# A left-shifted copy of the image: made on chip by POOL from the rows already loaded, in place of a second load

## The reference

```python
x = x + _L0_conv_ref(_gn(x), ...)   # normalise each channel, 3x3 depthwise conv with weights
                                    # chosen per image (softmax of 4 kernels), a sigmoid gate, 1x1 conv
x = x + _L1_conv_ref(_gn(x), ...)   # normalise, 1x1 conv to 192 channels, 3x3 depthwise, 8x8 FFT
                                    # product of q and k, layer norm, times v, 1x1 conv
```

## Time and profile before

| what | value |
|---|---|
| median of three runs | 3041.64 us (3037.79 to 3047.04) |
| the profiled execution's own time | 3043.07 us, of which 3041.0 us from the first to the last instruction |
| mean granted TensorE clock | 0.961 of full speed |
| PE, PEld, DVE, ACT, POOL busy | 88%, 55%, 67%, 73%, 19% |
| first stage | to about 676 us, 16 slots with a convolution |
| share of "DMA arena<-x_in" in the chain that ended last | 8% |

### The profile page before, as it was taken

How to read it: one execution, slowest core, us unless ns; L and a number is a source line. 1 busy time by engine, 2 the same in 40 slices (tenths; PEclk the granted TensorE clock), 3 DMA queues, 4 the chain that set the end, 5 groups by cost and what they waited for, 6 DMA issues and landing times.

```text
span 3041.0 us, 74966 instructions
## 1 busy us (share of the span) xinstructions
PE 2679.8 (88%) x28031; PEld 1676.5 (55%) x28031; DVE 2039.6 (67%) x3469; ACT 2219.4 (73%) x4445; POOL 574.6 (19%) x307
## 2 busy tenths in 40 slices
PE   2777777779999999999999999999999999999998
PEld 1222222226666666666666666666666666666665
DVE  7666666644767676666666667676666767676766
ACT  2455555558878787878787878787787878787885
POOL 4000000010222222222222222222222222222222
PEclk9898888879999999999999999999999999999999
DMA  9899999982222222223222222222222222222221
GB/s 190 203 283 276 287 271 270 270 212 66 59 59 58 59 58 59 69 63 72 62 69 63 68 59 58 59 58 59 59 58 59 58 59 58 59 58 59 58 58 42
DMA packets 43485, 313.88 MB, mean 103 GB/s; under 512 B 12913, under 2 KB 13050, under 8 KB 29658
## 3 DMA queue, kind: packets, MB, share of 16 engines
q1 hardware_dynamic: 43082, 308.58, 40.7%
HBM read 206.81 MB, written 101.72 MB: 101 GB/s over the span
## 4 chain that ended last, share of the span: by engine, by line
PE 60%; DVE 14%; ACT 9%; DMA 8%; issue 8%; SPq 1%; ACTq 0%; DVEq 0%; POOL 0%; POOLq 0%
PE bank L614 15%; PE bank L696 14%; PE bank L676 8%; DMA arena<-x_in 8%; PE bank L627 6%; PE bank L687 5%; PE bank L599 5%; PE bank L636 4%; DVE arena L1110 3%; ACT arena L862 3%; PE bank L562 2%; DVE arena L1130 2%; ACT arena L764 2%; DVE arena L1194 1%; DVE arena L1124 1%
## 5 line engine op out<-in xcount | busy, mean ns | idle before, releaser
L862 ACT ACTIVATE arena<-bank 64x256 f32<-64x256 f32 x2048 | 773.2, 378 | 141.0 <-PE bank L687 122.3
L486 POOL TENSOR_TENSOR arena<-arena 128x8 f32<-128x8 f32 x256 | 515.5, 2014 | 1833.8 <-DVE arena L1132 1833.7
L614 PE MATMUL bank<-arena 128*64 128x512 f16 x4608 | 715.2, 401 | 45.3 <-issue 45.3
L805 ACT ACTIVATE arena<-bank 100x512 f32<-100x512 f32 x1024 | 585.5, 639 | 105.5 <-PE bank L599 103.2
L1194 DVE TENSOR_TENSOR arena<-bank,arena 128x512 f32<-128x512 f32 x512 | 354.5, 692 | 455.4 <-ACT arena L862 410.4
L696 PE MATMUL bank<-arena 100*128 100x128 f32 x4096 | 590.0, 286 | 0.0
L696 PEld LDWEIGHTS bank<-arena 100*128 100x128 f32 x4096 | 495.8, 191 | 82.5 <-issue 82.5
L599 PEld LDWEIGHTS bank<-arena 128*64 128x64 f16 (+1 forms) x8192 | 340.4, 106 | 254.3 <-ACT arena L805 48.8
L599 PE MATMUL bank<-arena 128*64 128x128 f16 (+1 forms) x8192 | 414.4, 223 | 21.4 <-ACT arena L805 17.9
L562 PE MATMUL bank<-arena 128*32 128x512 f32 x3072 | 413.1, 679 | 4.7 <-DVE arena L986 4.0
L821 ACT ACTIVATE arena<-bank,arena 128x256 f32<-128x256 f32 x512 | 261.3, 561 | 138.5 <-PE bank L627 135.8
(11 more groups left out here) (122 smaller groups left out, 2133.1 us busy)
## 6 DMA issues: line engine op xcount, KB each, us to landing
arena<-xn_d SPq DMA_DIRECT2D x128, 536.2 KB, 8.9
xn_d<-arena SPq DMA_DIRECT2D x130, 260.0 KB, 14.1
arena<-x_in SPq DMA_DIRECT2D x64, 512.0 KB, 25.6
x_d<-arena SPq DMA_DIRECT2D x64, 512.0 KB, 14.7
arena<-x_d SPq DMA_DIRECT2D x128, 256.0 KB, 4.9
out<-arena SPq DMA_DIRECT2D x128, 256.0 KB, 4.4
arena<-x_in SPq DMA_DIRECT2D x16, 2047.9 KB, 26.9
arena<-spectra_in SPq DMA_DIRECT2D x1, 1152.0 KB
```

Of the source, the lines that this page charges most:

```text
L486: pool.tensor_tensor(tiny["rstd"][:, slot], tiny["var_eps"][:, slot], powers, ALU.pow).then_inc(s_root, 1)
L614: mm = pe.matmul(v_banks[chunk % 3][64 * s:64 * s + 64, :], v_w[:, 64 * tap:64 * tap + 64], at(xs[half], row * WP + 32 * k + dx, [32 * WP, ...
L805: act.activation(h_rows[0:WIN, :, first:first + 4], banks[g % ring][0:WIN, :].rearrange("p (i c) -> p c i", i=4), ACT.Copy).then_inc(s_h_r ...
L862: ins = act.activation(at(q_sb[n % 4][64 * to:64 * to + 64, :], 128 * half, [256, 2], [1, 128]), src, ACT.Copy)
```

## The change

The left load (`load_left`, its semaphores and its two issues on SP) is gone. POOL now waits for the middle load of `after` before it takes the root of `after`, and behind that root it makes the left-shifted copy itself: eight instructions of 16 rows by 127 columns over 32 partitions, from partitions 32 to 63 at one element further to partitions 64 to 95. The first is a multiplication by a row of ones, a two-input instruction, and the other seven are plain copies. Each adds one to `s_left_copied`. DVE's wait ahead of the edge memset (L1082) is for all eight in place of the left load. On POOL the copies stand behind the root of `after` and, in the first slot of all, behind `clear(1)`.

```diff
-        s_x3_left_in = [semaphore(f"x3_left_in{s}") for s in range(2)]
+        s_left_copied = semaphore("left_copied")
...
-            def load_left(b, n, s):
-
-                sp.dma_start(x3[s][64:96, W:W + PIX - 1], x[b].rearrange("c h w -> c (h w)")[:, 1:PIX]).then_inc(s_x3_left_in[s], 16)
...
                 if prev is not None:
-                    if after is not None:
-                        load_left(*after)
-                    elif here is not None:
+                    if after is None and here is not None:
                         load_transforms()
-                    else:
+                    elif after is None:
                         load_first_half()
                 elif after is not None:
                     b, n, s = after
                     load_middle(*after)
-                    load_left(*after)
...
                 if after is not None:
-                    root(after[0], 1)
+                    b, n, s = after
+                    pool.wait_ge(s_x3_mid_in[s], 16 * (n + 1))
+                    root(b, 1)
                     if prev is None and here is None:
                         clear(1)
+                    for i in range(8):
+                        first = (1 + 16 * i) * W
+                        dst, src = at(x3[s][64:96, :], first, [W, 16], [1, W - 1]), at(x3[s][32:64, :], first + 1, [W, 16], [1, W - 1])
+                        copied = pool.tensor_tensor(dst, src, at(ones_row[32:64, :], 0, [0, 16], [1, W - 1]), ALU.mult) if i == 0 else pool.tensor_copy(dst, src)
+                        copied.then_inc(s_left_copied, 1)
...
-                dve.wait_ge(s_x3_left_in[s], 16 * (n + 1))
+                dve.wait_ge(s_left_copied, 8 * (b + 1))
                 dve.memset(at(x3[s][64:96, :], 2 * W - 1, [W, H]), 0.0).then_inc(s_edges, 1)
```

## The result

| kernel | median | runs | ratio to the kernel before, 95% interval |
|---|---|---|---|
| before | 3044.34 us (3037.79 to 3052.52) | 4 | |
| after | 3109.78 us (3107.20 to 3112.95) | 4 | 1.0214 (1.0186 to 1.0242) |

The change costs 65 us. The profiled execution of after has a span of 3111.0 us, 70.0 more than that of before.

What follows compares the result with a forecast made beforehand. It took a chain through DVE's small operations to bound the slot. Thirteen slots 59.8, the first -1.6, the start +16.4 and +11.6 sum to +86 us: 3128 us, own range 3055 to 3190, whole range 3050 to 3235.

Steps and rivals of the forecast that it cites:

- What bounds the kernel: First-stage slot: a chain through DVE's small operations; DMA touches it at `xr` (1.04 us) and the edge memset (0.43 us).
- Durations: POOL's eight instructions: multiplication 3.4 us, each copy 1.9 us (1.72 to 3.4), a train of 16.7 us.
- the first rival: POOL's train: each copy takes 3.4 us, +12.5 us a slot, about +209 us, 3250 us in all; chance 0.12.
- Two-input DVE operations: DVE beside POOL's train: each waits for the whole present POOL instruction; the rows left between nothing and that.
- The slot by hand: One slot from the root's end: L530 +2.4 us, second right-shift copy +4.6, slot 4.6 us longer, 42.4 us.
- The first full slot: First of 14 slots with `prev` and `after`: 4.6 + 1.04 - 7.21, a change of -1.6 us.
- the wait for `xr`: DVE's statistics: the wait goes with the left load, -1.04 us a slot, 7.21 us in the first such slot.
- POOL's new wait: POOL ahead of the root of `after`: the middle load lands before the root's start, so it costs nothing.
- The start: Up to the first convolution: first matmul at 79.2 us against 62.76, +16.4 us; the next slot gains 11.6 us.
- The second stage: The 2360 us behind the first stage, which load no left copy: they keep their time, change 0.
- Uninterrupted POOL: POOL's train: DVE never gets between, L530 13.6 us late, about +212 us, 3255 us in all; chance 0.08.
- The other side: DVE's two-input operations and POOL's copies run side by side, L1017 on time, about -20 us, 3022 us; chance 0.12.

Runs made afterwards that it cites:

- e2_no_left: Changed kernel without its copies, so no left shift at all, the left-shifted partitions cleared once and kept zero: 3000.88 us, 0.9847 of the kernel before.
- e4_memset_train: Changed kernel with eight memsets of the same shape in place of POOL's eight copying instructions: 3102.23 us, 1.0159 of the kernel before.
- e1_plain_copies: Changed kernel with POOL's first instruction a plain copy and a one-element multiplication carrying the wait: 3073.30 us, 1.0087 of the kernel before.
- e9_half_start: Changed kernel, half the left shift by four plain copies, half by DMA; first slot's copies ahead of the root, long memset in 13 pieces: 3002.21 us, 0.9840.

## Why the prediction was right

The sign, the mechanism of the loss and its place were right: DVE's small operations wait for POOL's instructions. The size was 18 us too high against the median, 86 where the profile gives 70. A part of that nearness is luck: up to the second stage the forecast was 86 and the profiles give 61, and the 8.6 us of the second stage, forecast as 0, made up for a third of the difference.

- *What bounds the kernel.* Here a step failed: "a chain through DVE's small operations, with DMA touching it in two places". The greater touch is a third one, the middle load, whose 87.0 us of waiting on ACT the prediction read and set aside because PE waits only for DVE. It gave DMA's part 1.04 us a slot, through `xr`; e2_no_left gives 3.3, and its table shows all of it in the landing of the middle load.
- *Durations.* Copies: 1.9 us forecast, 12.81 us for seven in the first slot, so 1.83 each undisturbed. Multiplication: 3.4 forecast, 3.7 measured from start to start. The range's upper end of 3.4 a copy, and with it the first rival, is out.
- *Two-input DVE operations.* The trace of before was silent and I took the whole instruction. L1017's 3.67 us shows it, and e4_memset_train beside e1_plain_copies shows that a reading POOL instruction does it and a memset doesn't.
- *The slot by hand.* From the middle load's issue, forecast against the slot of after: multiplication ends 20.6 and 20.7; L1019 is done at 22.9 and 22.6; L530 23.2 and 22.6; L1051 done 33.9 and 32.7; the second right-shift copy done, 37.0 (510.2 plus its 1.21) and 35.6. The forecast was 0.6 us late at L530, 1.2 at L1051's end, 1.4 at that copy's end and 1.6 at the next issue. The term that was too large is the lateness handed on from L530 to L1051: this stretch took 10.14 us before and 8.88 after. Timelines of DVE and ACT in the slots of before and of after:

```profile
498.81 0.14 DVE L1029 COPY arena<-bank 128x1 f32<-128x1 f32 x1
```

```profile
500.19 0.19 ACT L772 ACTIVATE arena<-arena 128x1 f32<-128x1 f32 x1
```

```profile
508.00 0.14 DVE L1029 COPY arena<-bank 128x1 f32<-128x1 f32 x1
```

```profile
508.17 0.20 ACT L772 ACTIVATE arena<-arena 128x1 f32<-128x1 f32 x1 [3.81 <-DVE arena L1029]
```

  Before, ACT came to L772 1.24 us after DVE's L1029 was done, straight from its other work: DVE could be that much late at no cost. After, ACT stands 3.81 us and waits for L1029. The hand sum let this room out. It isn't the earlier middle load that shortens the stretch: in e2_no_left that lands as early as in after, and the stretch keeps its length (means of the twelve slots: 10.15 us before, 10.05 in e2_no_left, 8.93 after).
- *The first full slot.* -5.2 for -1.6. The forecast took the wait for `xr`. But the middle load landed 18.8 us after its issue in this slot of before and 12.3 in after, 6.4 us earlier, and that is the way which counts. POOL's new wait, booked at nothing, was 2.70 us long here, ahead of the root.
- *The start.* +14.5 us for the first convolution (77.22), forecast +16.4; +26.8 at the third middle load, forecast +28.0. Right. I let seven small operations wait; L1067, L1070, L1075 and L1077 took 3.54, 5.41, 5.46 and 1.92 us.
- *The second stage.* Forecast 0, measured +8.6. No line of it is touched. Its length in the eleven profiles lies between 2364.9 us (before) and 2377.0 (e9_half_start), and it is 2373.5 in e2_no_left, which has no copies, so nothing points to the copies. The four runs of the kernel before differ by 14.7 us among themselves, so 8.6 us between two single profiles can also be chance. The granted clock of the stretch is lower (windows view, 2361 us each; the column behind POOL is PEclk):

```profile
680.00:3041.00 2361.00, 2208.76 (x24612) 1515.34 (x24611) 1610.14 (x2432) 1868.44 (x4115) 515.52 (x256) 0.99 0.26 61
...
750.00:3111.00 2361.00, 2209.26 (x24593) 1517.00 (x24591) 1609.05 (x2430) 1862.68 (x4106) 515.54 (x256) 0.98 0.25 59
```

  The first is the kernel before, the second after. Why the clock is a little lower is open.
- *The rivals.* Uninterrupted POOL didn't happen with copies, though it exists with memsets. The other side needed L1017 to be free. What I didn't see is that the change contained a gain: with half the copies, placed in POOL's idle time, it is 1.3% faster.

## What to carry to other kernels

Work moved to POOL is not free because POOL is idle: ask which DVE operations fall into its time. A small one on the chain that starts behind a POOL copy costs that copy's whole length, and a row of them costs one each. Place such copies where DVE waits for another engine, keep each instruction short, and move only as much as the overloaded resource needs: dropping half the load was enough to bring the middle load's landing from 15.5 us to 12.4. A resource that is 98% busy can still be worth only part of its share; leave the work out once and measure what it gives. Then look for the one load that something on the chain waits for: here the slot was the middle load's landing plus 22.5 us, and only the landing moved.

## What the runs showed of the hardware

- A POOL copy of 32 by 2032 float32 takes 1.83 us (0.90 ns an element), nearly as little as a memset of that size (13.92 us for eight, 1.74 each). The two-input multiplication takes twice as much (3.7 us).
- DVE operations with two SBUF inputs wait for a POOL instruction that reads SBUF and not for one that only writes it. The Trainium skill states just this ("SBUF — State Buffer", section "Who interferes with whom"); the traces agree: the 128x1 operation L1019 took 1.74 to 1.79 us beside copies in e1_plain_copies and 0.22 us inside the memsets of e4_memset_train.
- A DVE copy that comes while memsets are queued on POOL can wait for all of them (14.59 us for eight, in e4_memset_train). Behind copies it waited for one (2.86 us at most in after, of which 1.21 are its own).
